# Token choice layer of a four-layer kernel: second weights in four pieces, another place for two stores and for the split of x

## The chip, the cores and the metric

The program runs on 1 core of one Trainium2 chip. The metric is the device time of one execution in microseconds (us).

## The reference, cut to what matters

Four layers work on x of shape (8, 1024, 256), float32: windowed attention, a token choice layer with 64 small experts, linear attention, and attention with nested widths; each is followed by a residual sum and a layer norm. The change touches the second one only:

```python
grouped = x.reshape(x.shape[:-2] + (-1, 16, d))          # groups of 16 tokens
logits = jnp.einsum('...btd,des->...btes', grouped, controller) + tie
perm = (logits == jnp.max(logits, axis=-3, keepdims=True)).astype(x.dtype)
sel = jnp.einsum('...btd,...btes->...besd', grouped, perm)   # 64 experts pick one token each of a group
inner = jax.nn.relu(jnp.einsum('...besd,desf->...besf', sel, f1) + bias)
inter = jnp.einsum('...besf,esfd->...besd', inner, f2)       # f2: 64 experts of 64 x 256
out = jnp.einsum('...besd,...btes->...btd', inter, perm)     # back to the tokens
x = _layernorm(x + out)
```

## The kernel before

The engines are TensorE (PE), VectorE (DVE), ScalarE (ACT) and GpSimd (POOL). SP issues the DMAs of this layer, in its program order; a wait in front of one DMA holds up all behind it. Every engine walks through one list of steps, `steps`, written out by hand. A step is (offset, kind, number); in the turn B of the list it works on the pair of sequences X = B + offset. There are four pairs, X = 0 to 3, and turns for B from -1 to 4; a step whose pair does not exist is left out. What a step does on each engine stands in the functions `piece`. An engine runs its parts in the order of the list, so the list sets the order on all five.

A pair has 2048 tokens in 128 groups. The 64 experts are worked through in two halves of 32. For one half:

- `pT` (L1252) transposes the one-hot choice; ACT copies it to `chosen` (L1123).
- `sel` (L1261) multiplies x by the choice. x is split into two parts, `hi` and `lo`, both in the buffer `hl`: ACT writes hi = x rounded (L1131), then lo = x - hi (`low`, L927) follows, on POOL for pairs 1 to 3. For pair 0 DVE makes the first half of lo and POOL the second, at the end of the layer ahead.
- `h` (L1267) applies the first weights f1, ACT (L1159) and DVE (L1192) add the bias and clip into `hidden`; two `h` steps a half.
- `inter` (L1274), eight steps a half, applies f2 to four experts each. ACT (L1163) and DVE (L1197) evacuate half each into `wide`, and SP stores each of these outputs, 0.5 MB, to DRAM (L1062).
- `gather` (L1075) reads the half's eight outputs back in another layout, in four pieces of 1 MB, once all eight stores have landed.
- `out` (L1281), four steps a half, brings them back to the tokens; DVE adds them to x (L1207) and for half 1 takes the statistics (L176).

PE's results go to four PSUM slots in rotation; a slot is reused when its readers are done.

After half 1 of a pair, `aggregate` (DVE L182, then POOL L187 and L189, the reciprocal root) and `rescale` normalise x: DVE scales the second eight tiles in four steps, POOL the first eight in one (L932). POOL makes the copies of step (0, "spread", 1) (L1103) before it. `store` (L1079) writes a half of x to the next layer, 1 MB each: store 1 needs DVE's tiles, store 0 POOL's.

The next pair is prepared beside half 1 of the present one: `load` of x in two halves (L1056), `xT` (PE L957, copies L975), `logits` (PE L969), then on DVE the tie (L949), the maximum (L938) and the comparison with it (L940), for half 0 at once and for half 1 in step `second`. `spread` 0 (ACT L1143) lays the choice out for `pT`.

The tile names of the profile are those of a buffer's first name: `l0f_f` in the layer is f2 (in DRAM `in_dram`), `l0f_hl` is hi and lo, `x` in DRAM is the layer's input or output.

f2 has one buffer of 2 MB for 32 experts, `f2`. Half 0 of a pair needs the first 32 experts, half 1 the others, so it is loaded twice a pair, each time in one DMA (L1069), when the eighth `inter` of the half before has been filled. `inter` 0 and `inter` 8 wait for it.

Of the kernel before, what the change touches and what calls it, by code (L numbers as in the profile page):

```python
# [49 lines left out]


def tokens(dram, b):

    return dram[bass.ds(b, 1), :, :].rearrange("o (t p) d -> p (o t) d", p=P)


def alone(eng):


    eng.nop(nofuse=True)  # L60


def wait_alone(eng, sem, value):
    eng.wait_ge(sem, value)
    alone(eng)
# [754 lines left out]
def token_choice_layer(nc, block, semaphores, kept, x_in, y_out, controller, f1_in, f2_in, f1_bias, tie_in, ident_in, scratch):  # L820
# [13 lines left out]
    PAIRS = EH // 2  # L834
    HB = 8
    IN = PAIRS // 2
    NC = TT // 4
    NB = NSEQ // 2
    def selection(half):
        out = [(0, "pT", half * TP)]  # L840
        for tp in range(TP):
            if tp + 1 < TP:
                out.append((0, "pT", half * TP + tp + 1))
            out.append((0, "sel", half * TP + tp))
        return out

    def experts(half):
        h, o = [(0, "h", 2 * half + n) for n in range(2)], [(0, "inter", IN * half + n) for n in range(IN)]
        return [h[0], o[0], o[1], h[1]] + o[2:]

    def combination(offset, half):
        return [(offset, "out", NC * half + n) for n in range(NC)]

    s, e, late = selection(0), experts(0), combination(-1, 1)
    turned = selection(1)[:2]
    steps = [(-1, "gather", 1), (0, "f2", 0)] + s[2:] + e[:1] + late + [(-1, "aggregate", 0), (0, "spread", 1)]
    steps += e[1:4] + [(-1, "rescale", 0), e[4], (-1, "rescale", 1), e[5], (-1, "rescale", 2), e[6], (-1, "rescale", 3), e[7], turned[0],
                       e[8], turned[1], e[9]]
    steps += [(-1, "store", 1), (-1, "store", 0), (0, "gather", 0), (1, "load", 0), (1, "load", 1), (0, "f2", 1)]
    s, e, early = selection(1), experts(1), combination(0, 0)  # L860
    steps += s[2:] + e[:1] + early + [(1, "xT", n) for n in range(4)] + [(1, "logits", 0), (1, "spread", 0)]
    steps += e[1:4] + [(1, "second", 0)] + e[4:6] + [(1, "hi", 0), (1, "lo", 0)] + e[6:8]
    steps += [(1, "hi", 1), (1, "lo", 1), (1, "pT", 0), e[8], (1, "pT", 1), e[9]]
    slotted = ("xT", "logits", "pT", "sel", "h", "inter", "out")

    sb, _, sem = allocators(nc, kept, semaphores, "l0f", "right")
    consts = sem("consts"); setup = sem("setup")
    ln = LayerNorm(sb, sem, "ln", setup, 1, TT)
    spread = sb("spread", [P, 2, NQ, J, G])
    x = sb("x", [P, 2, TT, D])  # L870
    wide = sb("wide", [P, 2 * TT, D])
    xT = wide[:, 0:TT, :].rearrange("p t d -> p (t d)").rearrange("p (c t) -> p c t", c=CH)
# [8 lines left out]
    hi, lo = (hl[:, part, :, :].bitcast(f32r) for part in range(2))  # L881
    hidden = sb("hidden", [P, 8, NG])
    f2 = sb("f2", [P, PAIRS, D])
    f1 = sb("f1", [P, CH, E, F])
    schedule = Schedule(steps, slotted, None, NB)
    arrived = schedule.arrived

    def signal(name, per, step=1):
        return Signal(sem(name), per, step)

    f1_loaded = sem("f1_loaded"); f2_loaded = signal("f2_loaded", 2, 16)
    x_loaded = [signal(f"x_loaded{n}", 1, 16) for n in range(2)]; stored = [signal(f"stored{n}", 1, 16) for n in range(2)]
    filled = {o: signal(f"filled{o - schedule.offsets[0]}", sum(s[0] == o for s in schedule.plan))
              for o in schedule.offsets}
# [8 lines left out]
    left = [signal(f"left{half}", IN, 16) for half in range(2)]  # L903
    normed = [signal(f"normed{n}", NT) for n in range(2)]
    back = [signal(f"back{i}", 2, 16) for i in range(NC)]
# [13 lines left out]
    f2_rows = f2_in.rearrange("(p e) f d -> (e f) p d", e=2)  # L919
# [57 lines left out]
    class First:  # L977
# [10 lines left out]
            return buffer[(slice(None),) * (len(names.split()) + 1)].rearrange(f"p {names} -> p ({names})")  # L988

        def start_sp(self, sp):  # L990
            for s in (f2_loaded, *x_loaded, *stored, *left, *back):
                s.start(sp)

        def start_pool(self, pool):
# [47 lines left out]
    def programs(tail, sb, ps):  # L1042
# [3 lines left out]
        @block.sync  # L1046
        def _(sp):
            def piece(step, X, seq, n, B):
                _, kind, i = step
                part = slice(NT * i, NT * i + NT)  # L1050
                if kind == "load" and X:
                    if X == 1:
                        tail.wait_stored(sp)
                    stored[i].wait(sp, X - 2)
                    alone(sp)
                    x_loaded[i].by(sp.dma_start(x[:, X % 2, part, :], tokens(x_in, 2 * X + i)))  # L1056
                if kind == "inter":
                    half, n = divmod(i, IN)
                    inter_even.wait(sp, X, i + 1)
                    alone(sp)  # L1060
                    inter_odd.wait(sp, X, i + 1)
                    left[half].by(sp.dma_start(scratch[half, :, 4 * n:4 * n + 4, :], wide[:, 4 * n:4 * n + 4, :]))  # L1062
                if kind == "f2":
                    schedule.wait_filled(sp, X if i else X - 1, ("inter", IN - 1 if i else 2 * IN - 1))
                    alone(sp)
                    if X == 0 and i == 0:
                        for sem, count in tail.read:
                            wait_alone(sp, sem, count)
                    f2_loaded.by(sp.dma_start(f2[:, :, :], f2_rows[:, PAIRS * i:PAIRS * i + PAIRS, :]))  # L1069
                if kind == "gather":  # L1070
                    wait_alone(sp, left[i].sem, (X + 3) * IN * 16)
                    rows = scratch[i, :, :, :].rearrange("(q j) e d -> (j e) q d", j=J)
                    for n in range(NC):
                        q = slice(NQ // NC * n, NQ // NC * (n + 1))
                        back[n].by(sp.dma_start(wide[:, q, :], rows[:, q, :]))  # L1075
                if kind == "store":
                    normed[i].wait(sp, X)
                    alone(sp)
                    stored[i].by(sp.dma_start(tokens(y_out, 2 * X + i), x[:, X % 2, part, :]))  # L1079

            schedule.loop(sp, piece)

        @block.gpsimd
# [131 lines left out]
        def _(pe):  # L1215
# [6 lines left out]
            def piece(step, X, seq, n, B):  # L1222
                _, kind, i = step
# [12 lines left out]
                if kind == "inter":  # L1236
                    hidden_even.wait(pe, X, 2 * i + 2)
                    hidden_odd.wait(pe, X, 2 * i + 2)
                    if i % IN == 0:
                        f2_loaded.wait(pe, X, i // IN + 1)  # L1240
                if kind == "out":
                    back[i % NC].wait(pe, X, i // NC + 1)
                s = schedule.use(pe, X, step, B)
# [4 lines left out]
                if kind == "pT":  # L1248
                    half, tp = divmod(i, TP)
# [26 lines left out]
                if kind == "out":  # L1276
                    half, n = divmod(i, NC)
# [923 lines left out]
```

How the kernel before makes its waits and increments, by code:

```python
def wait_alone(eng, sem, value):  # L63
    eng.wait_ge(sem, value)
    alone(eng)
# [37 lines left out]
    def wait(self, eng, block, n=None):  # L103
        eng.wait_ge(self.sem, self.count(block, n))
# [27 lines left out]
    def wait_free(self, pe, b, key):  # L133
        old = self.before(key)
        if old is not None:
            for sem, per_sequence, position in self.emptied(old):
                pe.wait_ge(sem, b * per_sequence + position)
# [44 lines left out]
    def reciprocal_root(self, pool, b, use):  # L184
        pool.wait_ge(self.aggregated, self.count(b, use) * self.tiles)
        pool.tensor_scalar(self.mv[:, :, 1], self.mv[:, :, 1], LN_EPS, None, ALU.add).then_inc(self.var_ready, 1)
        pool.wait_ge(self.var_ready, self.count(b, use))
        pool.tensor_tensor(self.rstd[:, :], self.mv[:, :, 1], self.half[:, :], ALU.pow).then_inc(self.rstd_ready, 1)
# [45 lines left out]
    def wait_memsets(self, eng):  # L235
        eng.wait_ge(self.setup, 3)
# [15 lines left out]
def negative_mean(pool, ln, to, sems, X):  # L252
    pool.wait_ge(ln.rstd_ready, X + 1)
    pool.tensor_tensor(to[:, :], ln.mv[:, :, 0], ln.rstd[:, :], ALU.mult).then_inc(sems[0], 1)
    pool.wait_ge(sems[0], X + 1)
    pool.tensor_scalar(to[:, :], to[:, :], -1.0, None, ALU.mult).then_inc(sems[1], 1)
# [43 lines left out]
    def use(self, pe, X, step, B):  # L301
# [5 lines left out]
        if i > -4 * size:  # L307
            for sem, count in self.until(B + i // size, self.plan[i % size]):
                pe.wait_ge(sem, count)
        return self.slot_in(B, step)
# [649 lines left out]
    def logits(pe, X, s):  # L960
        if X == 0:
            pe.wait_ge(consts, 16 * NCONST)
        xT_even.wait(pe, X)
```

## Time and profile before

| what | value |
|---|---|
| median of 3 runs | 2532.25 us (2531.35 to 2538.84) |
| the profiled execution: its time | 2531.27 us |
| the profiled execution: span of the core | 2529.4 us |
| token choice layer within the span | about 1030 to 1450 us |
| PE busy over the span | 2190.4 us, 87% |
| DVE, ACT, POOL busy | 1419.5, 994.7, 899.1 us |

The span runs from the first to the last instruction; the execution's own time has 1.9 us more around it. An engine counts as busy while it computes; its waits and the issuing of DMAs do not count.

### The profile page before, as it was taken

How to read it: one execution, taken by the hardware profiler on the slowest of the kernel's cores; microseconds unless marked ns; L12 is line 12 of the kernel's file. 1: busy time of each engine (PE TensorE's matmuls, PEld its weight loads, DVE VectorE, ACT ScalarE, POOL GpSimd, SP SyncE). 2: the span in 40 equal slices, each digit the busy share in tenths (PEclk: the TensorE clock that was granted, in tenths of full speed). 3: DMA queues.
4: the chain of work that ended last, by engine and by line, in shares of the span. 5: the costliest groups of instructions: out<-in, count | busy, mean ns of one | idle time of the engine just before them, and what ended most of it. 6: DMA issues, size and time to landing. Idle time of an engine off the chain costs nothing.

```text
span 2529.4 us, 42561 instructions
## 1 busy us (share of the span) xinstructions
PE 2190.4 (87%) x17140; PEld 1376.5 (54%) x17140; DVE 1419.5 (56%) x2526; ACT 994.7 (39%) x1450; POOL 899.1 (36%) x573
## 2 busy tenths in 40 slices
PE   4899999999999999788878599999588888888885
PEld 2445555555555555566667456776355555555553
DVE  3545555555555555556466444554466777676772
ACT  1233333333333333545435144333144554554443
POOL 4222222222222220103123022201457877787784
PEclk7899999999999999999999899999799999999997
DMA  6555555555555554367877722201663455445411
GB/s 150 117 118 110 109 110 110 109 115 110 113 110 116 110 107 89 125 212 261 280 248 266 263 92 67 67 26 33 190 161 99 114 145 145 132 113 146 128 35 50
DMA packets 227971, 328.81 MB, mean 130 GB/s; under 512 B 14544, under 2 KB 167104, under 8 KB 227520
## 3 DMA queue, kind: packets, MB, share of 16 engines
q1 hardware_dynamic: 220784, 321.49, 48.4%
q10 hardware_dynamic: 6992, 4.60, 0.6%
q8 instruction: 137, 2.24, 0.4%
q14 instruction: 58, 0.48, 0.1%
HBM read 197.46 MB, written 127.93 MB: 129 GB/s over the span
## 4 chain that ended last, share of the span: by engine, by line
PE 57%; DVE 16%; POOL 7%; DMA 7%; ACT 5%; issue 4%; SPq 3%; ACTq 1%; POOLq 0%; DVEq 0%
PE l0a_slot L775 8%; PE l0a_slot L785 7%; PE l0a_O L710 5%; DVE l1f_rowmax L1972 4%; PE l1a_slot L1568 4%; PE l0a_slot L752 4%; POOL l1f_added L1849 4%; ACT l0f_f L590 2%; PE l0a_slot L757 2%; PE l1a_slot L1559 2%; PE l0a_slot L803 2%; POOL l1f_added L1851 2%; DVE l0f_hidden L655 2%; DMA l0f_f<-in_dram 2%; PE l1f_slot L2103 2%
## 5 line engine op out<-in xcount | busy, mean ns | idle before, releaser
L590 ACT ACTIVATE l0f_f<-l0a_slot 128x1024 f32<-128x1024 f32 (+1 forms) x256 | 248.3, 971 | 337.8 <-PE l0a_slot L775 189.0
L655 DVE TENSOR_REDUCE l0f_hidden<-l0a_slot 128x4 f32<-128x1024 f32 (+1 forms) x256 | 293.4, 1156 | 115.5 <-PE l0a_slot L785 112.5
L1921 ACT ACTIVATE l1f_probs<-l1f_slot 128x1024 f32<-128x1024 f32 x240 | 243.8, 1022 | 271.9 <-PE l1f_slot L2103 265.2
L1849 POOL TENSOR_TENSOR l1f_added<-l1f_probs 128x1024 f32<-128x1024 f32 x117 | 277.3, 2370 | 152.4 <-ACT l1f_probs L1921 152.4
L1972 DVE TENSOR_REDUCE l1f_rowmax<-l1f_slot 128x1 f32<-128x1024 f32 x240 | 287.2, 1216 | 65.6 <-PE l1f_slot L2094 64.9
L775 PE MATMUL l0a_slot<-l0f_hidden 128*128 128x512 bf16 (+1 forms) x1024 | 296.0, 374 | 13.3 <-DMA l0f_hl<-qk_rows 9.0
L549 POOL TENSOR_TENSOR l0f_x<-l0f_x 128x512 f32<-128x512 f32 x32 | 40.7, 1272 | 540.3 <-DVE l0f_x L639 540.3
L2103 PE MATMUL l1f_slot<-l1f_Qs,l1f_Ks 128*128 128x256 f32 x960 | 173.9, 306 | 39.0 <-DVE l1f_lo L1962 14.8
L2103 PEld LDWEIGHTS l1f_slot<-l1f_Qs,l1f_Ks 128*128 128x128 f32 x960 | 146.3, 198 | 96.9 <-DVE l1f_rowmax L1972 33.9
L2094 PE MATMUL l1f_slot<-l1f_Ks,l1f_Qs 96*128 96x512 f32 x480 | 175.9, 451 | 25.7 <-DVE l1f_rowmax L1972 18.4
L710 PE MATMUL l0a_O<-l0f_f,l0f_wide 128*32 128x128 f32 x3840 | 156.4, 279 | 10.5 <-issue 10.5
L1851 POOL TENSOR_TENSOR l1f_added<-l1f_added 128x512 f32<-128x512 f32 x117 | 149.6, 1279 | 9.2
L2027 PE MATMUL l1f_os<-l1f_probs,l1f_V 128*32 128x256 f32 x1920 | 145.4, 396 | 0.1
L785 PE MATMUL l0a_slot<-l0a_Qs,l0f_hl 49*128 49x256 f32 (+1 forms) x1024 | 127.1, 327 | 18.3 <-ACT l0f_f L590 17.1
L785 PEld LDWEIGHTS l0a_slot<-l0f_hl,l0a_Qs 48*128 48x128 f32 x1024 | 77.7, 188 | 103.8 <-issue 103.8
L785 PEld LDWEIGHTS l0a_slot<-l0a_Qs,l0f_hl 49*128 49x128 f32 x1024 | 76.8, 186 | 103.3 <-issue 68.3
L752 PE MATMUL l0a_slot<-l0f_x,l0f_spread 128*128 128x512 f32 x256 | 123.5, 629 | 6.6 <-DVE l0f_spread L623 5.1
L785 PE MATMUL l0a_slot<-l0f_hl,l0a_Qs 48*128 48x256 f32 (+1 forms) x1024 | 128.7, 330 | 0.0
L710 PEld LDWEIGHTS l0a_O<-l0f_f,l0f_wide 128*32 128x32 f32 x3840 | 90.3, 109 | 64.6 <-issue 37.4
L775 PEld LDWEIGHTS l0a_slot<-l0f_hidden 128*128 128x128 bf16 x1024 | 63.8, 98 | 96.5 <-issue 61.7
L2094 PEld LDWEIGHTS l1f_slot<-l1f_Ks,l1f_Qs 96*128 96x128 f32 x480 | 78.3, 199 | 68.8 <-issue 30.0
L601 ACT COPY l0f_f<-l0a_O 128x512 f32<-128x512 f32 x64 | 37.4, 585 | 196.1 <-PE l0a_O L710 196.0
(194 smaller groups left out, 3770.2 us busy)
## 6 DMA issues: line engine op xcount, KB each, us to landing
expert_outputs<-l0f_wide SPq DMA_DIRECT2D x64, 512.0 KB, 3.3
l0f_wide<-expert_outputs SPq DMA_DIRECT2D x32, 1024.0 KB, 10.9
l1f_Ks<-kq_rows SPq DMA_DIRECT2D x48, 512.0 KB, 8.2
l0a_Qs<-qk_rows SPq DMA_DIRECT2D x90, 256.0 KB, 7.8
l0f_hl<-qk_rows SPq DMA_DIRECT2D x90, 256.0 KB, 14.5
l0f_f<-in_dram SPq DMA_DIRECT2D x10, 2048.0 KB, 14.7
qk_rows<-l0f_wide SPq DMA_DIRECT2D x32, 512.0 KB, 2.8
qk_rows<-l0f_x SPq DMA_DIRECT2D x32, 512.0 KB, 4.2
```

The source lines that it names most:

```text
L590: exp_ready.by(act.activation(probs[:, t % 2, HG * g:HG * g + HG, 0:reach, :], s[:, :, 0:reach, :], ACT.Exp, scale=SCALE))
L655: max_ready.by(dve.reduce_max(rowmax[:, t, :, 2 * g:2 * g + 2], s[:, :, :, first:2 * P], AX))
L710: last = mm(O[t % 2][32 * j:32 * j + 32, g, :], V[:, tile - a, HG * g + j, :], probs[:, (t - a) % 2, HG * g + 2 * (j % 2) + j // 2, a, :], ...
L752: last = mm(s[:, BW * r:BW * r + BW], w[:, c, P * r:P * r + P], xT[:, n, c, :], start=c == 0, stop=c == CH - 1)
L775: at_end = mm(o[:, half, :, reach, :], ident16[:, :], table[:, reach, :].unsqueeze(1).broadcast_to([P, 2, wide, P]), start=not mask_ends, ...
L785: last = mm(o[:, half, j, reach, :].rearrange("p a q -> p (a q)"), left[r, 2 * g + j, here], right[r, 2 * g + j, moving], start=mask_ends ...
L1849: halved.by(pool.tensor_tensor(added[:, u, :], probs[:, 0, u, :], probs[:, 1, u, :], ALU.add))
L1851: add_done.by(pool.tensor_tensor(added[:, u, 0:SKT * QW], added[:, u, 0:SKT * QW], added[:, u, SKT * QW:HKT * QW], ALU.add))
L1921: exp_done.by(act.activation(probs[:, half, u - FIRST[b], :], s[:, :], ACT.Exp, scale=SCALE))
L1972: max_done.by(dve.reduce_max(rowmax[:, i:i + 1], s[:, :], AX))
L2094: last = mm(s[:, 512 * half:512 * half + 512], Qs[0:96, parity, u, P * t:P * t + P], Ks[0:96, parity, UNITS[u][0], 512 * half:512 * half + ...
L2103: last = mm(s[:, QW * j:QW * j + QW], Ks[:, parity, UNITS[u][0], P * kt:P * kt + P], Qs[:, parity, u, :], start=True, stop=True)
```

## The change

f2 is loaded in four pieces of 0.5 MB a half, step numbers 0 to 3 for half 0 and 4 to 7 for half 1, each with a semaphore of its own (`f2_loaded[part]`). A piece may be loaded when the second `inter` step that reads its predecessor in the buffer has been filled, and every second `inter` step waits for its piece. Two pieces of each half go out among the `inter` steps of the half before, the other two behind the gather (and behind the loads of x). The stores of the old pair move: store 1 from behind `inter` 7 to before `inter` 6 (`e[8]`), store 0 to before `inter` 7 (`e[9]`). The steps `hi` and `lo` of the next pair move from between the `inter` steps of half 1 to directly behind `logits`, before `spread` 0.

```diff
--- before.py
+++ after.py
@@ -853,14 +853,14 @@
 
     s, e, late = selection(0), experts(0), combination(-1, 1)
     turned = selection(1)[:2]
-    steps = [(-1, "gather", 1), (0, "f2", 0)] + s[2:] + e[:1] + late + [(-1, "aggregate", 0), (0, "spread", 1)]
-    steps += e[1:4] + [(-1, "rescale", 0), e[4], (-1, "rescale", 1), e[5], (-1, "rescale", 2), e[6], (-1, "rescale", 3), e[7], turned[0],
-                       e[8], turned[1], e[9]]
-    steps += [(-1, "store", 1), (-1, "store", 0), (0, "gather", 0), (1, "load", 0), (1, "load", 1), (0, "f2", 1)]
+    steps = [(-1, "gather", 1), (0, "f2", 2), (0, "f2", 3)] + s[2:] + e[:1] + late + [(-1, "aggregate", 0), (0, "spread", 1)]
+    steps += e[1:4] + [(0, "f2", 4), (-1, "rescale", 0), e[4], (-1, "rescale", 1), e[5], (0, "f2", 5), (-1, "rescale", 2), e[6],
+                       (-1, "rescale", 3), e[7], turned[0], (-1, "store", 1), e[8], turned[1], (-1, "store", 0), e[9]]
+    steps += [(0, "gather", 0), (1, "load", 0), (1, "load", 1), (0, "f2", 6), (0, "f2", 7)]
     s, e, early = selection(1), experts(1), combination(0, 0)
-    steps += s[2:] + e[:1] + early + [(1, "xT", n) for n in range(4)] + [(1, "logits", 0), (1, "spread", 0)]
-    steps += e[1:4] + [(1, "second", 0)] + e[4:6] + [(1, "hi", 0), (1, "lo", 0)] + e[6:8]
-    steps += [(1, "hi", 1), (1, "lo", 1), (1, "pT", 0), e[8], (1, "pT", 1), e[9]]
+    steps += s[2:] + e[:1] + early + [(1, "xT", n) for n in range(4)] + [(1, "logits", 0)]
+    steps += [(1, "hi", 0), (1, "lo", 0), (1, "hi", 1), (1, "lo", 1), (1, "spread", 0)]
+    steps += e[1:4] + [(1, "f2", 0), (1, "second", 0)] + e[4:6] + [(1, "f2", 1)] + e[6:8] + [(1, "pT", 0), e[8], (1, "pT", 1), e[9]]
     slotted = ("xT", "logits", "pT", "sel", "h", "inter", "out")
 
     sb, _, sem = allocators(nc, kept, semaphores, "l0f", "right")
@@ -888,7 +888,7 @@
     def signal(name, per, step=1):
         return Signal(sem(name), per, step)
 
-    f1_loaded = sem("f1_loaded"); f2_loaded = signal("f2_loaded", 2, 16)
+    f1_loaded = sem("f1_loaded"); f2_loaded = [signal(f"f2_loaded{n}", 2, 16) for n in range(4)]
     x_loaded = [signal(f"x_loaded{n}", 1, 16) for n in range(2)]; stored = [signal(f"stored{n}", 1, 16) for n in range(2)]
     filled = {o: signal(f"filled{o - schedule.offsets[0]}", sum(s[0] == o for s in schedule.plan))
               for o in schedule.offsets}
@@ -988,7 +988,7 @@
             return buffer[(slice(None),) * (len(names.split()) + 1)].rearrange(f"p {names} -> p ({names})")
 
         def start_sp(self, sp):
-            for s in (f2_loaded, *x_loaded, *stored, *left, *back):
+            for s in (*f2_loaded, *x_loaded, *stored, *left, *back):
                 s.start(sp)
 
         def start_pool(self, pool):
@@ -1061,12 +1061,13 @@
                     inter_odd.wait(sp, X, i + 1)
                     left[half].by(sp.dma_start(scratch[half, :, 4 * n:4 * n + 4, :], wide[:, 4 * n:4 * n + 4, :]))
                 if kind == "f2":
-                    schedule.wait_filled(sp, X if i else X - 1, ("inter", IN - 1 if i else 2 * IN - 1))
+                    half, part = divmod(i, 4)
+                    schedule.wait_filled(sp, X if half else X - 1, ("inter", 2 * part + 1 if half else IN + 2 * part + 1))
                     alone(sp)
                     if X == 0 and i == 0:
                         for sem, count in tail.read:
                             wait_alone(sp, sem, count)
-                    f2_loaded.by(sp.dma_start(f2[:, :, :], f2_rows[:, PAIRS * i:PAIRS * i + PAIRS, :]))
+                    f2_loaded[part].by(sp.dma_start(f2[:, 4 * part:4 * part + 4, :], f2_rows[:, 4 * i:4 * i + 4, :]))
                 if kind == "gather":
                     wait_alone(sp, left[i].sem, (X + 3) * IN * 16)
                     rows = scratch[i, :, :, :].rearrange("(q j) e d -> (j e) q d", j=J)
@@ -1236,8 +1237,8 @@
                 if kind == "inter":
                     hidden_even.wait(pe, X, 2 * i + 2)
                     hidden_odd.wait(pe, X, 2 * i + 2)
-                    if i % IN == 0:
-                        f2_loaded.wait(pe, X, i // IN + 1)
+                    if i % 2 == 0:
+                        f2_loaded[i % IN // 2].wait(pe, X, i // IN + 1)
                 if kind == "out":
                     back[i % NC].wait(pe, X, i // NC + 1)
                 s = schedule.use(pe, X, step, B)
```

## Rows read from the trace of the kernel before

**Rows 1.** The page, busy time of the engines over the whole span.

```profile
PE 2190.4 (87%) x17140; PEld 1376.5 (54%) x17140; DVE 1419.5 (56%) x2526; ACT 994.7 (39%) x1450; POOL 899.1 (36%) x573
```

**Rows 2.** Busy times in one stretch; the last number is GB/s of the DMA queues.

```profile
1102.50:1122.00 19.50, 15.26 (x151) 11.11 (x150) 8.44 (x15) 3.92 (x11) 0.00 (x0) 0.91 1.07 348
```

**Rows 3.** Waits of PE from 1030 to 1440 us: total us, times, longest.

```profile
PE l0f_slot L1274 <- DMA l0f_f<-in_dram: 10.8, 3, 4.1
...
PE l0f_slot L1261 <- ACT l0f_chosen L1123: 7.7, 4, 2.4
```

**Rows 4.** Timeline of PE: start us, us; in brackets the idle time before.

```profile
1122.67 1.94 PE L957 MATMUL l0f_slot<-l0f_ident,l0f_x 128*128 128x128 f32 x16 [1.07 <-DMA l0f_x<-x]
...
1220.87 1.94 PE L957 MATMUL l0f_slot<-l0f_ident,l0f_x 128*128 128x128 f32 x16 [1.07 <-DMA l0f_x<-x]
...
1243.96 1.75 PE L1261 MATMUL l0f_slot<-l0f_chosen,l0f_hl 128*128 128x256 f32 x8 [2.36 <-ACT l0f_chosen L1123]
...
1269.59 2.00 PE L1274 MATMUL l0f_slot<-l0f_f,l0f_hidden 64*128 64x256 f32 x16 [2.56 <-DMA l0f_f<-in_dram]
...
1316.11 1.94 PE L957 MATMUL l0f_slot<-l0f_ident,l0f_x 128*128 128x128 f32 x16 [1.08 <-DMA l0f_x<-x]
...
1411.19 3.47 PE L1274 MATMUL l0f_slot<-l0f_f,l0f_hidden 64*128 64x256 f32 x16 [4.12 <-DMA l0f_f<-in_dram]
```

**Rows 5.** Timeline of the queue SP, the issues of the gathers.

```profile
1100.68 5.65 SPq L1075 DMA_DIRECT2D l0f_wide<-expert_outputs  x4
...
1195.63 9.77 SPq L1075 DMA_DIRECT2D l0f_wide<-expert_outputs  x4
...
1247.59 5.44 SPq L1075 DMA_DIRECT2D l0f_wide<-expert_outputs  x4
...
1291.04 9.76 SPq L1075 DMA_DIRECT2D l0f_wide<-expert_outputs  x4
```

**Rows 6.** Timeline of POOL.

```profile
1056.61 4.84 POOL L927 TENSOR_TENSOR l0f_hl<-l0f_x,l0f_hl 128x2048 fp32r<-128x2048 f32 x1 [12.98 <-ACT l0f_hl L1131]
...
1062.72 2.81 POOL L1103 COPY l0f_spread<-l0f_choice 32x512 f32<-32x512 f32 x4
...
1182.09 10.02 POOL L932 TENSOR_SCALAR l0f_x<-l0f_x,l0f_ln_mv,l0f_ln_rstd 128x256 f32<-128x256 f32 x8 [0.24 <-POOL l0f_spread L1103]
...
1239.33 9.06 POOL L927 TENSOR_TENSOR l0f_hl<-l0f_x,l0f_hl 128x2048 fp32r<-128x2048 f32 x2 [47.22 <-ACT l0f_hl L1131]
...
1280.55 9.95 POOL L932 TENSOR_SCALAR l0f_x<-l0f_x,l0f_ln_mv,l0f_ln_rstd 128x256 f32<-128x256 f32 x8 [0.24 <-POOL l0f_spread L1103]
```

**Rows 7.** Timeline of DVE.

```profile
1043.73 1.38 DVE L195 TENSOR_SCALAR l0f_x<-l0f_x,l0a_ln_mv,l0a_ln_rstd 128x256 f32<-128x256 f32 x4 [1.55 <-POOL l0a_ln_rstd L189]
...
1054.76 2.29 DVE L927 TENSOR_TENSOR l0f_hl<-l0f_x,l0f_hl 128x2048 fp32r<-128x2048 f32 x1 [3.31 <-ACT l0f_hl L1131]
...
1062.87 2.81 DVE L195 TENSOR_SCALAR l0f_x<-l0f_x,l0a_ln_mv,l0a_ln_rstd 128x256 f32<-128x256 f32 x4 [2.76 <-POOL l0a_ln_rstd L189]
...
1229.93 0.69 DVE L940 TENSOR_TENSOR l0f_choice<-l0f_choice,l0f_best 128x512 f32<-128x512 f32 x1
...
1272.92 1.17 DVE L182 BATCH_NORM_AGGREGATE l0f_ln_mv<-l0f_ln_stats 128x2 f32<-128x6 f32 x16
...
1285.85 0.69 DVE L1197 COPY l0f_wide<-l0f_slot 128x512 f32<-128x512 f32 x1 [1.25 <-PE l0f_slot L1274]
```

**Rows 8.** Timeline of ACT.

```profile
1050.27 2.54 ACT L1143 COPY l0f_spread<-l0f_choice 32x512 f32<-32x512 f32 x4 [1.70 <-DVE l0f_choice L940]
...
1230.71 2.53 ACT L1143 COPY l0f_spread<-l0f_choice 32x512 f32<-32x512 f32 x4 [7.73 <-DVE l0f_choice L940]
...
1237.32 1.93 ACT L1131 CAST l0f_hl<-l0f_x 128x2048 fp32r<-128x2048 f32 x1
```

**Rows 9.** DMA issues from 1030 to 1440 us: count, size, us to landing.

```profile
expert_outputs<-l0f_wide SPq DMA_DIRECT2D x64, 512.0 KB, 3.3
...
x<-l0f_x SPq DMA_DIRECT2D x6, 1024.0 KB, 6.5
```
## The prediction

> **What bounds the kernel now.** I read the page first: TensorE (PE) is busy for 87% of the whole span [rows 1], so a gain must come from stretches where PE stands still. The change touches the token choice layer alone, about 1030 to 1450 us. The table of waits for this layer comes next [rows 3]: PE waits 10.8 us for the second weights (f2) and 7.7 us in front of the selection matmuls, besides its waits for gathered outputs and for x. These are the waits that the change aims at; which of them carry time is read from the timelines [rows 4 to 8].
>
> I cut the layer at the moments at which the second half of x lands and PE turns it: 1122.67, 1220.87 and 1316.11 [rows 4]. One full turn, 1220.87 to 1316.11, is 95.2 us and has four links. (a) 53.2 us until VectorE (DVE) has aggregated the statistics of the old pair, 1272.92+1.17 = 1274.1 [rows 7]. (b) 16.4 us until GpSimd (POOL) ends its root, its copies and eight rescaled tiles, 1280.55+9.95 = 1290.5 [rows 6]. (c) 0.5 us until the queue issues gather 0 at 1291.04 [rows 5]. (d) 25.1 us until x has landed behind it [rows 4]. The turn before it took 98.2 us, since gather 0 left 3.5 us after POOL's end (1192.1 to 1195.63) and x 25.2 us later [rows 4 to 6]. The last turn runs from 1316.11 to 1411.19, where the first output matmul of half 1 waits 4.12 us for f2 [rows 4].
>
> On an idle queue gather 0 is quicker: issued at 1100.68, with x there at 1122.67, it is 22.0 us for 6 MB [rows 4, 5]. At the 348 GB/s that the queue then moves [rows 2], 1 MB takes 3.0 us; so the fourth piece of a gather lands 22.0-6.0 = 16.0 us after the issue, and the backlog of the two y stores is worth 25.1-22.0 = 3.1 us.
>
> **The change, part by part.**
>
> **f2 in pieces, half 0.** PE no longer waits for f2 before expert output 0 (2.56 us at 1269.59, 10.8 us in three waits [rows 3, 4]). I cost this gain at nothing by itself: the outputs' evacuations stand behind the aggregate in DVE's order, and the aggregate runs until 1274.1, after f2 is there [rows 7]. It needs the gathered outputs, not f2. If DVE were free it would be worth up to 2.6 us a turn. The 4.12 us before 1411.19 are on the path and counted below. With them goes the half-speed stretch behind that wait: sixteen matmuls took 3.47 us there, against 2.00 us after the shorter wait at 1269.59 [rows 4]; -1.6 us with what follows it.
>
> **f2 in pieces, the load added elsewhere.** Two pieces of 0.5 MB now go out between the eight output stores of each half, 1.5 us each. The first falls into the gap left by the h step and costs nothing; the second falls among stores back to back and makes the gather 1.5 us later. For pair 0, half 0 that is +1.5 us on x (0 to +3). For the other halves it is in the numbers below.
>
> **x split behind the logits, pair 0.** ScalarE (ACT) is idle 1.70 us before its spread, which starts at 1050.27, and makes hi only after its 2.54 us [rows 8]. Now hi comes first, from 1048.6, so done at 1050.4 and 1052.3. DVE makes lo 0 (2.29 us) from 1051.5 to 1053.8; POOL's lo 1 follows, and its end moves from 1061.45 to 1058.4 if POOL must let DVE finish, or to 1057.3 if not [rows 6, 7]. POOL's root, the last normalisation of the layer ahead and the selection's evacuations follow that end: -3.0 us (-4.1 without a conflict; 0 if another chain takes over).
>
> **x split behind the logits, pairs 1 to 3.** ACT stands idle 7.73 us before its spread at 1230.71 [rows 8]; hi 0 and hi 1 (1.93 us each) fit there, from 1223.0 to 1226.8. So 3.9 us leave the loaded part of ACT's order, and selection no longer waits for lo 0, which POOL now ends at 1239.33+4.53 = 1243.9, just where PE resumes at 1243.96 [rows 4, 6]. That wait of 2.36 us is gone, and it is the gain one would expect.
>
> But POOL's two lo's now run from 1225.0 to 1229.5 and from there to 1234.1. DVE's comparison (L940: two operands, both in SBUF) wants to start at 1229.93 [rows 7], 0.4 us into the second. The trace has no such comparison under a lo. Nearest is the normalisation L195: four tiles take 1.38 us with POOL idle, and 2.81 us while POOL makes four copies, which take 2.81 us too [rows 6, 7]. The two engines took turns, one whole instruction each. The other overlap is lo 1 of pair 0, started 0.44 us before DVE's lo 0 ended: 4.84 us instead of 4.53 [rows 6, 7]. Bounds for L940: no delay, or the rest of lo 1, 4.2 us. I take 4.2 us, by L195. The Trainium skill (SBUF — State Buffer, Who interferes with whom) says the same of just this pair of instructions: a DVE instruction with two SBUF inputs and a GpSimd instruction that reads SBUF exclude each other for a whole instruction, and the later one waits. By it, too, the delay is 4.2 us; were it wrong here, the sum would be that of rival 1.
>
> With 4.2 us the first stores of half 1 are 4.2 us later. The f2 piece adds 1.5 us; gather 1 goes out near 1253.4 instead of 1247.59 [rows 5]. Its fourth piece lands 16.0 us later, at 1269.4; PE's last combination ends near 1271.3, and DVE's add (1.2), statistics (1.4) and aggregate (1.2) at 1275.1. Link (a) is then +1.0 us in each of three turns. Without the delay, ACT's shorter order brings the last store forward and gather 1 goes out near 1249.3: fourth piece 1265.3, aggregate end 1271.0, so -3.1 us a turn.
>
> **y stores ahead of the last outputs.** Store 1 needs DVE's tiles only and moves forward freely. Store 0 needs POOL's eight tiles, which end at 1290.5 [rows 6], while DVE has evacuated output 7 at 1285.85+0.69 = 1286.5 [rows 7], as POOL's end hangs on the aggregate alone. The queue works in order: behind store 0 stand now the store of output 7, gather 0, both loads of x and the last f2 pieces, and PE waits for them. Before, output 7 had landed when POOL finished. Now 1 MB and 0.5 MB go out at POOL's end, and gather 0 must wait until the latter has landed. A 1 MB y store lands after 6.5 us, an output store after 3.3 us [rows 9]; with 1.5 us of data for output 7 the pair takes between 6 and 9 us. I take 7.5. After POOL's end x then needs 7.5+22.0 = 29.5 us, against 28.8 before in the first turn (+0.7) and 25.6 in the second (+3.9). In the third, half 1 starts when the fourth combination (1.95 us) is through: 7.5+16.0+1.95 = 25.4 against some 25.5 (-0.1; this contains the 4.12 us wait for f2). Together +4.5 us; each us on the 7.5 counts three times. The Trainium skill (DMA: Bandwidth & Descriptors, Queues, rings and completion order) adds that a DMA's semaphore increment lands only after all earlier writes of that engine; by it the store of output 7 can't be seen before store 0 has been written, which keeps the lower end near 6.
>
> **Sum:** -3.0 (pair 0) +1.5 (first gather) +3x1.0 +4.5 -1.6 = +4.4 us. The profiled execution took 2531.27 us (span 2529.4 and 1.9 around it), 1.0 below the median of 2532.25. So 2535.7 for that execution, and 2536.6 as a median.
>
> **The rivals.**
> 1. *No delay of L940* (it is served beside lo 1, or comes 0.4 us before it). Then -4.1+1.5-3x3.1+4.5-1.6 = -9.0: 2523.2 us, faster. For it: no row shows this pair of instructions, and the margin is small. Against it: the L195 and lo 1 rows.
> 2. *The store of output 7 lands later*: queued behind f2 piece 5, store 1, output 6 and store 0, it needs 10 us after POOL's end instead of 7.5. Price 3x2.5: 2544.1 us, slower. It decides from about 8.6 us on, since +4.4+3x1.1 is 7.6 us. For it: outputs 2 to 6, the f2 piece and store 1 are 4 MB, 12 us of data asked for in the 11 us before POOL's end. Against it: a median landing of 6.5 us that already has backlog in it [rows 9].
> 3. *The change does what it says*: every f2 wait and selection wait is gain, 10.8+7.7 us: 2513.8 us. Against it: both end behind work of DVE and POOL. It has no chance of its own beyond 0.03.
>
> **How the numbers follow.** 0.3% of the time, 7.6 us, is about what a measurement tells from no change. Forecast 0.50 (its own range 2530 to 2543), rival 1 0.27, rival 2 0.20, rival 3 0.03. Of the forecast 0.42 stays within the bound and 0.06 lies above it; rival 1 gives 0.17 faster and 0.10 within; rival 2 0.18 slower; the rest is split. Faster 0.21, same 0.54, slower 0.25. The range reaches to both rivals: 2520 to 2545.
>
> **What would show it.** Right: L940 ends near the end of POOL's second lo in pairs 1 to 3, and ACT's spread follows; no f2 wait on PE; on the queue a gap before output 7's store until POOL's last tile, and gather 0 some 7 us after POOL's end; selection of pair 0 about 3 us earlier. Wrong: L940 at its old distance from the logits; aggregates 3 us earlier; gather 0 within 5 us of POOL's end; or DVE's normalisation ahead of pair 0 not moved.

## The result, and the profile after

| | median | runs | ratio to before, 95% interval |
|---|---|---|---|
| before | 2535.01 us | 8 (2530.90 to 2538.84) | |
| after | 2543.94 us | 8 (2539.32 to 2544.74) | 1.0035 [1.0024, 1.0045] |

The change makes the kernel 8.9 us slower, 6 to 11 us by the interval. The profiled execution after has a span of 2541.5 us. The numbers of the lines below 859 are one higher in the kernel after (L1274 is L1275, L1281 is L1282, L1131 is L1132).

The page of the kernel after, the engines' busy time, answers to [rows 1]:

```profile
PE 2196.1 (86%) x17140; PEld 1373.5 (54%) x17140; DVE 1432.1 (56%) x2526; ACT 994.7 (39%) x1450; POOL 900.2 (35%) x573
```

PE runs the same 17140 matmuls and is busy 5.7 us longer with them; the other 6.4 of the 12.1 us more of span are waits. DVE is busy 12.6 us longer, and that is not work either: 11.6 us of it are three rows of one instruction, shown below. PE's waits from 1030 to 1440 us answer to [rows 3]:

```profile
PE l0f_slot L1282 <- DMA l0f_wide<-expert_outputs: 31.9, 23, 2.7
PE l0f_slot L1275 <- ACT l0f_wide L1164: 10.4, 3, 3.5
```

The wait for f2 has gone, and so has the one in front of the selection, as the change promises. In their place stand a wait for ACT's evacuations, 3.5 us in each of three turns, and more waiting for the gathered outputs: before it was 24.0 us, but 11.6 of them in one wait at 1436.47, whose counterpart of 12.2 us ends at 1445.55 in the kernel after, outside this window, so 12.4 us have become 31.9. The timelines of one turn show where each comes from. First DVE, with the pair's first maximum, the comparison and the aggregate ([rows 7] before):

```profile
1229.36 0.68 DVE L938 TENSOR_REDUCE l0f_best<-l0f_choice 128x32 f32<-128x512 f32 x1
1230.07 4.54 DVE L940 TENSOR_TENSOR l0f_choice<-l0f_choice,l0f_best 128x512 f32<-128x512 f32 x1
...
1275.54 1.17 DVE L182 BATCH_NORM_AGGREGATE l0f_ln_mv<-l0f_ln_stats 128x2 f32<-128x6 f32 x16
```

The comparison L940 took 0.69 us before and takes 4.54 us now. I read this as waiting inside the row and not as slower computing; e1 and e9 below test it. POOL in the same stretch ([rows 6] before), from pair 0's lo on:

```profile
1050.22 5.80 POOL L927 TENSOR_TENSOR l0f_hl<-l0f_x,l0f_hl 128x2048 fp32r<-128x2048 f32 x1 [8.62 <-ACT l0f_hl L1132]
...
1225.01 9.05 POOL L927 TENSOR_TENSOR l0f_hl<-l0f_x,l0f_hl 128x2048 fp32r<-128x2048 f32 x2 [34.05 <-ACT l0f_hl L1132]
...
1283.09 10.04 POOL L932 TENSOR_SCALAR l0f_x<-l0f_x,l0f_ln_mv,l0f_ln_rstd 128x256 f32<-128x256 f32 x8 [0.24 <-POOL l0f_spread L1104]
```

The two lo's run from 1225.01 to 1234.06. The comparison begins at 1230.07, some 0.5 us after the start of the second lo, and its row ends at 1234.61, 0.55 us after the end of that lo. Behind it ACT's spread and evacuations ([rows 8] before):

```profile
1223.02 3.70 ACT L1132 CAST l0f_hl<-l0f_x 128x2048 fp32r<-128x2048 f32 x2
1234.70 2.53 ACT L1144 COPY l0f_spread<-l0f_choice 32x512 f32<-32x512 f32 x4 [7.97 <-PE l0f_slot L1275]
1237.26 1.07 ACT L1164 COPY l0f_wide<-l0f_slot 128x512 f32<-128x512 f32 x2
```

hi now takes its 3.70 us in ACT's idle time, but the spread starts at 1234.70, 3.9 us later after x than before (1230.71). PE, turn by turn ([rows 4] before):

```profile
1221.01 1.94 PE L957 MATMUL l0f_slot<-l0f_ident,l0f_x 128*128 128x128 f32 x16 [1.08 <-DMA l0f_x<-x]
...
1238.09 4.64 PE L1275 MATMUL l0f_slot<-l0f_f,l0f_hidden 64*128 64x256 f32 x24 [3.45 <-ACT l0f_wide L1164]
...
1323.19 1.94 PE L957 MATMUL l0f_slot<-l0f_ident,l0f_x 128*128 128x128 f32 x16 [1.07 <-DMA l0f_x<-x]
```

The bracket at 1238.09 is the wait that has come: PE stands 3.45 us for an evacuation behind the spread. The queue ([rows 5] before):

```profile
1254.79 5.42 SPq L1076 DMA_DIRECT2D l0f_wide<-expert_outputs  x4
...
1287.62 0.58 SPq L1080 DMA_DIRECT2D x<-l0f_x  x1
...
1293.19 0.37 SPq L1080 DMA_DIRECT2D x<-l0f_x  x1
1293.66 0.87 SPq L1062 DMA_DIRECT2D expert_outputs<-l0f_wide  x1
1301.00 5.35 SPq L1076 DMA_DIRECT2D l0f_wide<-expert_outputs  x4
```

Gather 1 goes out at 1254.79, 33.8 us after x has landed at 1221.01 (26.7 before). Store 0 goes out when POOL has finished its eighth tile at 1293.13, the store of output 7 at 1293.66 behind it, and gather 0 only at 1301.00, 7.9 us after POOL's end (0.5 before). The chain of waits links these up:

```profile
1245.64 0.70 DVE l0f_wide L1198
1246.35 1.16 SPq L1062
...
1247.60 7.12 DMA expert_outputs<-l0f_wide
...
1257.44 13.29 DMA l0f_wide<-expert_outputs
...
1270.78 1.97 PE l0f_slot L1282 x16
1272.77 1.23 DVE l0f_x L1208
...
1283.09 10.05 POOL l0f_x L932 x8
...
1293.66 7.28 DMA expert_outputs<-l0f_wide
...
1311.33 11.72 DMA l0f_x<-x
```

The last output of half 1 takes 7.12 us to land, the last output of half 0 7.28 us; POOL's tiles stand between the aggregate and the queue. The start of the last half, without the f2 wait that stood before it:

```profile
1421.29 2.00 PE L1275 MATMUL l0f_slot<-l0f_f,l0f_hidden 64*128 64x256 f32 x16
1423.22 3.71 PE L1268 MATMUL l0f_slot<-l0f_sel,l0f_f 128*64 128x128 f32 x64
```

### The profile page after: what moved, and what is told of

Same layout as the page of the kernel before. It is cut to its first block, busy times and chain, and to the rows that moved or that the text cites. A ratio compares the mean times of both kernels' runs of the same rounds, so it can differ in the third digit from the quotient of the medians.

```text
span 2541.5 us, 42619 instructions
## 1 busy us (share of the span) xinstructions
PE 2196.1 (86%) x17140; PEld 1373.5 (54%) x17140; DVE 1432.1 (56%) x2526; ACT 994.7 (39%) x1450; POOL 900.2 (35%) x573
## 4 chain that ended last, share of the span: by engine, by line
PE 56%; DVE 15%; POOL 9%; DMA 7%; ACT 5%; issue 4%; SPq 3%; ACTq 1%; POOLq 0%; DVEq 0%
PE l0a_slot L775 8%; PE l0a_slot L785 7%; PE l0a_O L710 5%; DVE l1f_rowmax L1973 4%; PE l1a_slot L1569 4%; PE l0a_slot L752 4%; POOL l1f_added L1850 4%; DMA l0f_wide<-expert_outputs 3%; ACT l0f_f L590 2%; PE l0a_slot L757 2%; DMA expert_outputs<-l0f_wide 2%; PE l1a_slot L1560 2%; PE l0a_slot L803 2%; POOL l1f_added L1852 2%; DVE l0f_hidden L655 2%
## 5 line engine op out<-in xcount | busy, mean ns | idle before, releaser
L2104 PEld LDWEIGHTS l1f_slot<-l1f_Qs,l1f_Ks 128*128 128x128 f32 x960 | 145.3, 196 | 95.4 <-DVE l1f_rowmax L1973 32.5
```

The source lines that it names most:

```text
L2104: last = mm(s[:, QW * j:QW * j + QW], Ks[:, parity, UNITS[u][0], P * kt:P * kt + P], Qs[:, parity, u, :], start=True, stop=True)
```

## The experiments

All turns were cut as in the prediction. (a) is x landed to aggregate end, (c) POOL's end to gather 0, (d) gather 0 to the next x; (b), aggregate to POOL's end, is 16.2 to 16.5 us in every kernel. "Pair 0" is from the start of the last projection of the layer ahead (L803) to x of pair 1, "g1" from x landed to the issue of gather 1. The turn shown is the second, in us; each number is a difference of two starts or ends in the one profiled execution of that kernel, which can lie some us beside the median (e2: 2540.5 against 2534.9, e7: 2523.3 against 2527.1). The medians are of 4 to 12 runs; each ratio is to runs of the kernel before that were taken beside that kernel, with medians of 2533.0 to 2535.0 us.

| kernel | pair 0 | g1 | (a) | (c) | (d) | median | ratio to before |
|---|---|---|---|---|---|---|---|
| before | 73.95 | 26.7 | 53.2 | 0.5 | 25.1 | 2535.0 | 1 |
| after | 71.96 | 33.8 | 55.7 | 7.9 | 22.2 | 2543.9 | 1.0035 |
| e5 split alone | 70.72 | 31.8 | 53.4 | 7.7 | 24.7 | 2545.8 | 1.0045 [1.0032, 1.0058] |
| e6 stores alone | 73.25 | 26.6 | 51.8 | 8.7 | 21.1 | 2541.2 | 1.0027 [1.0016, 1.0038] |
| e7 f2 alone | 75.46 | 29.5 | 51.8 | 2.8 | 24.3 | 2527.1 | 0.9974 [0.9963, 0.9984] |
| e4 split in old place | 75.56 | 30.2 | 53.2 | 7.6 | 22.3 | 2538.5 | 1.0010 [0.9999, 1.0022] |
| e1 lo 1 waits | 72.20 | 30.4 | 52.2 | 7.8 | 21.9 | 2531.8 | 0.9984 [0.9973, 0.9994] |
| e2 store 0 back | 72.00 | 34.7 | 57.1 | 4.8 | 23.3 | 2534.9 | 0.9997 [0.9985, 1.0009] |
| e3 both | 72.49 | 30.1 | 51.9 | 5.3 | 22.1 | 2523.4 | 0.9947 [0.9930, 0.9964] |
| e9 lo 1 after first comparison | 72.32 | 30.2 | 51.8 | 5.4 | 21.8 | 2522.0 | 0.9952 [0.9935, 0.9969] |
| e8 both stores behind | 72.64 | 29.7 | 51.8 | 3.3 | 23.6 | 2521.8 | 0.9954 [0.9941, 0.9967] |
| e10 one f2 piece early | 70.80 | 28.3 | 50.2 | 3.3 | 22.5 | 2510.0 | 0.9906 [0.9891, 0.9921] |
| e11 same, both stores behind | 70.77 | 27.9 | 49.8 | 1.2 | 24.7 | 2513.4 | 0.9922 [0.9907, 0.9937] |
| e12 e10 with old split | 72.47 | 28.3 | 53.1 | 3.8 | 22.2 | 2524.3 | 0.9962 [0.9948, 0.9976] |

My theory after the result: two costs, the comparison standing outside POOL's second lo, in link (a), and the queue standing in front of output 7's store, in link (c). The rivals: each long row or wait costs nothing, since something else sets the turn.

**e1: the second lo waits for both comparisons.** An edit on the kernel after, in POOL's piece:

```diff
                 if kind == "lo" and X:
+                    if i:
+                        choice_ready.wait(pool, X)
                     low(pool, X, i)
```

> The kernel after, with one wait more: GpSimd starts the second half of lo only when VectorE has made both comparisons of the pair (the first half of lo starts as early as in the kernel after). Theory (the comparison of 4.54 us is VectorE standing outside GpSimd's second lo, and it delays everything of half 1 behind it): the first comparison is back at 0.69 us, gather 1 goes out 4 to 6 us earlier after x, and each of three turns is 3 to 5 us shorter, so 2543.9 - 12 = about 2532 us, ratio to the kernel before 0.996 to 1.001. Rival A (a long row that costs nothing, since the stores of output 7 behind store 0 set the turn): unchanged, ratio 1.003 to 1.004. Rival B (the moved wait only shifts the collision to the second comparison or delays the selection): comparison rows of over 1 us appear elsewhere, ratio above 1.002.

All comparisons take 0.69 us again. Gather 1 goes out 3.4 us earlier in the turn shown (4.5 and 3.9 in the others), link (a) is 3.5 us shorter (55.7 to 52.2), and the time falls to 2531.8 us, 12 us below the kernel after. The collision cost that much; rivals A and B fall.

**e2: store 0 behind inter 7 again.** On the kernel after:

```diff
-    ... e[8], turned[1], (-1, "store", 0), e[9]]
-    steps += [(0, "gather", 0), ...
+    ... e[8], turned[1], e[9]]
+    steps += [(-1, "store", 0), (0, "gather", 0), ...
```

> The kernel after, with store 0 behind inter 7 again, directly ahead of gather 0; store 1 stays ahead of inter 6. Theory (the queue stands 5 us before the store of output 7 until GpSimd's last tile, then waits for its landing behind 1 MB): gather 0 goes out under 2 us after GpSimd's end instead of 7.8 to 8.2; x lands some 23 to 25 us after that end instead of 30.1, so three turns are each 4 to 6 us shorter: about 2529 us, ratio 0.996 to 1.000. Rival A (the data queue is full anyway, so store 0 costs its 3 us behind the gather what it costs ahead of it): at most 2 us a turn, ratio 1.001 to 1.003.

A gain of 9 us over the kernel after, a part of it from (c): 4.8 us instead of 7.9. That is not the "under 2 us" of the theory. The second turn's (c) and (d) together are 28.0 us against 30.1, the 2 us a turn that rival A allowed at most, though its ratio (1.001 or more) was too high: the gather does not go out when POOL is through, but when output 7 has landed, 8.06 us after its store at 1291.05. The whole 9 us can't be followed in the profile, since the profiled execution was the slowest of the twelve.

**e3: both edits.**

> Both edits on the kernel after: the second half of lo waits for both comparisons, and store 0 stands behind inter 7. Theory: the two costs lie in different links of the turn (x to the aggregate, and GpSimd's end to x) and add up, so 2543.9 - 12 - 15 = about 2517 us, ratio 0.991 to 0.996. Rival (they lie in series on one resource, the DMA queue, and removing one exposes the other's cost elsewhere): no better than the better of the two alone, ratio 0.997 or more.

2523.4 us, a ratio of 0.9947, within the expected band, though 6 us above the expected 2517, which had counted 15 us for the stores where e2 gives 9; (a) shows the one gain and (c) the other. They add up (12.1 and 9.0 us alone, 20.5 us together) and the rival falls. The chain of waits of this kernel, at output 7, shows what is left in (c):

```profile
1278.45 8.31 DMA expert_outputs<-l0f_wide
...
1286.83 0.37 SPq L1076
```

Output 7 takes 8.31 us to land. Ahead of it on the queue are an f2 piece and store 1, behind it store 0.

**e4: the split back in its old place,** all else as after. The edit puts `(1, "hi", 0), (1, "lo", 0)` behind e[4:6] and the other two behind e[6:8] again.

> The kernel after, with the steps hi and lo back between the inter steps of half 1. Theory: the comparisons take 0.69 us again, but ScalarE's 3.9 us of hi and the wait of the selection for lo are back too, and so is the later start of pair 0 (3.4 us). Each of three turns 1 to 3 us shorter than in the kernel after, minus 3.4 us at pair 0: 2537 to 2543 us, ratio 1.001 to 1.003. Rival (the early split gained nothing at all, its cost was pure): ratio 0.998 or below.

2538.5 us, as expected: comparisons of 0.69 us, but pair 0 is 3.6 us later (75.56 against 71.96).

**e5: the early split alone,** on the kernel before.

> The kernel before with one part of the change alone: hi and lo of the next pair directly behind logits. Theory: the first comparison takes 4.5 us in pairs 1 to 3, gather 1 goes out 4 us later after x and f2 lands behind it; pair 0 starts 3.4 us earlier. 2535 to 2541 us, ratio 1.000 to 1.002. Rival (the early split is a gain in itself and only the mixture with f2 and the stores hurts): ratio 0.998 or below.

The largest miss: 2545.8 us, no faster than the whole change (the intervals, 1.0032 to 1.0058 and 1.0024 to 1.0045, overlap). The theory priced it too low, and the rival had the wrong sign. PE's timeline of this kernel, the fourth combination of the half is the first row:

```profile
1268.34 1.95 PE L1281 MATMUL l0f_slot<-l0f_wide,l0f_spread 128*64 128x256 f32 x16 [1.07 <-DMA l0f_wide<-expert_outputs]
1274.38 3.79 PE L1274 MATMUL l0f_slot<-l0f_f,l0f_hidden 64*128 64x256 f32 x16 [4.09 <-DMA l0f_f<-in_dram]
```

The gather is 5.1 us later after x than before, and f2, still in one DMA behind it, lands 4 us after PE has finished the combinations. The matmuls behind that wait are slow too: sixteen in 3.79 us against 2.00 us, with a granted clock of 0.66 from 1274.4 to 1282.6, so a part of it at the lower level of 1.2 GHz. Output 7 is evacuated at 1292.9, after POOL's end at 1290.5, and (c) is 7.7 us although no store stands in its way. In the kernel before, PE resumed at 1269.59 behind its f2 wait of 2.56 us, output 7 was evacuated at 1286.5 and (c) was 0.5 us. I read it so that POOL's tiles hid the lateness there and no longer hide it here; no run separates the late gather from the late f2.

**e6: the two stores alone,** on the kernel before.

> The kernel before with one part alone: store 1 ahead of inter 6, store 0 ahead of inter 7. Theory: the queue stands in front of the store of output 7 until GpSimd's last tile and the gather goes out 7 us after it; x lands 29 to 30 us after GpSimd's end (28.8 and 25.6 before). Together +6 to +10 us: 2541 to 2545 us, ratio 1.002 to 1.004. Rival (the y stores' 3.1 us of backlog saved behind the gather pay for it, as the run with store 0 moved back suggests with 2 us a turn): ratio 0.999 to 1.0015.

2541.2 us, as the theory has it: (c) is 8.7 us, and (d) is 4.0 us shorter without the backlog. In the first turn (c) is 9.7 us. One thing was not in the theory: (a) is 51.8 us in the turn shown and 53.2 in the other two, with the split in its old place in all three. PE waits about 2.36 us in front of the selection in each; behind that wait eight matmuls took 1.19 us in the turn shown:

```profile
1248.14 1.19 PE L1261 MATMUL l0f_slot<-l0f_chosen,l0f_hl 128*128 128x256 f32 x8 [2.36 <-ACT l0f_chosen L1123]
```

In the kernel before they took 1.75 us at 1243.96 [rows 4] and the next eight 2.06 us, with a granted clock of 0.57 from 1243.9 to 1247.9 against 1.00 in e6 from 1248.1 to 1252.1. The two levels of 1.2 and 2.4 GHz thus make (a) 53.0 to 53.2 or 51.8 to 51.9 us where the selection decides; no run tells why the clock fell in some turns and not in others.

**e7: f2 in pieces alone,** on the kernel before.

> The kernel before with one part alone: f2 in four pieces a half. Theory: no wait for f2, the last turn some 4 us and the stretch behind it 1.6 us shorter; against that 1.4 us on the first gather and about 1 us a turn for the piece among the stores. 2528 to 2534 us, ratio 0.9975 to 1.000. Rival (every wait for f2 of the kernel before is gain, 12.6 us with the two that end with it): ratio 0.9955 or below.

2527.1 us, a gain of 0.26%, just below the 2528 to 2534 expected. The rival, that each wait for f2 is gain, would have given 0.9955 or below and falls. In this execution the clock held behind all three waits for the selection (eight matmuls in 1.19 us), and (a) is 0.8 to 1.4 us shorter than before; that part need not be f2's doing. The three parts alone are +0.45, +0.27 and -0.26%, together +0.46% against the measured +0.35%: nearly additive.

**e8: lo 1 waits, both y stores behind inter 7.**

> The kernel after with the second lo waiting for both comparisons and both y stores behind inter 7, as in the kernel before. In the run with store 0 alone put back the gather still went out 5.3 us after GpSimd's end, as the store of output 7 took 8.3 us to land with 1 MB of store 1 and an f2 piece ahead of it. Theory (that backlog is store 1's, and it costs the same 3 us ahead of the gather as behind it): the gather goes out 1 to 3 us after GpSimd's end, x lands 24 to 25 us behind it, and the time is that of the run with both fixes, 2521 to 2526 us, ratio 0.9945 to 0.9965. Rival (store 1 ahead is a gain of its own): ratio above 0.9965.

2521.8 us, the same as e3. Behind output 7's store, store 1 takes 2.0 us off (c) (5.3 to 3.3) and adds 1.5 us to (d) (22.1 to 23.6); its place does not measurably matter so long as POOL is not in front of the queue.

**e9: as e3, but the second lo waits for the first comparison alone** (`choice_ready.wait(pool, X, 1)`).

> The kernel with both fixes, but the second lo waits for the first comparison alone, so it starts just when that comparison ends and is over before the second one wants to start (GpSimd's lo takes 4.5 us, the comparisons lie 6.9 us apart). Theory (only the overlap of a comparison with a running lo costs): all comparisons 0.69 us, the time that of the run with both fixes, 2519 to 2527 us, ratio 0.993 to 0.997. Rival (any lo on GpSimd in this stretch slows VectorE, which also adds, evacuates and clips there): rows of VectorE under the second lo longer than before, ratio above 0.998.

POOL and DVE of this kernel:

```profile
1218.43 4.55 POOL L927 TENSOR_TENSOR l0f_hl<-l0f_x,l0f_hl 128x2048 fp32r<-128x2048 f32 x1 [31.14 <-ACT l0f_hl L1134]
1224.26 4.55 POOL L927 TENSOR_TENSOR l0f_hl<-l0f_x,l0f_hl 128x2048 fp32r<-128x2048 f32 x1 [1.28 <-DVE l0f_choice L940]
```

```profile
1223.49 0.69 DVE L940 TENSOR_TENSOR l0f_choice<-l0f_choice,l0f_best 128x512 f32<-128x512 f32 x1
...
1230.35 0.69 DVE L940 TENSOR_TENSOR l0f_choice<-l0f_choice,l0f_best 128x512 f32<-128x512 f32 x1
```

The second lo starts 0.08 us after the first comparison ends. It overlaps two of DVE's copies (1.28 us) and six of its clips (1.71 us), which read PSUM and take just as long as in e3; it is over at 1228.81, before DVE's second maximum and comparison. 2522.0 us, the time of e3: the overlap with the comparison costs, the overlap with the copies and clips does not.

**e10: as e3, with one f2 piece early instead of two.** Pieces 1 and 5 go behind the gather (and the loads of x) with the other two:

```diff
-    steps = [(-1, "gather", 1), (0, "f2", 2), (0, "f2", 3)] + ...
+    steps = [(-1, "gather", 1), (0, "f2", 1), (0, "f2", 2), (0, "f2", 3)] + ...
-    ... e[5], (0, "f2", 5), (-1, "rescale", 2) ...
+    ... e[5], (-1, "rescale", 2) ...
-    ... (1, "load", 1), (0, "f2", 6), (0, "f2", 7)]
+    ... (1, "load", 1), (0, "f2", 5), (0, "f2", 6), (0, "f2", 7)]
-    ... e[4:6] + [(1, "f2", 1)] + e[6:8] ...
+    ... e[4:6] + e[6:8] ...
```

> The kernel with both fixes, and of the four f2 pieces of a half only the first goes out among the inter steps ahead; the second goes behind the gather with the other two. Theory (a piece among back-to-back stores delays the landing of the last store by its 1.5 us, and nobody needs the second piece before 20 us after the gather's issue): gather 1 goes out 1 to 1.5 us earlier after x, gather 0 as much earlier after GpSimd's end, six to seven such places: 2514 to 2520 us, ratio 0.992 to 0.995. Rival (the queue has slack there, the landing of the last store is set by its evacuation): unchanged, 2523 us, ratio 0.9945 to 0.996.

2510.0 us, 13 us below e3 and better than expected. Pair 0, g1 and (c) are 1.7, 1.8 and 2.0 us shorter (1.4 and 2.2, 1.4 and 1.7 in the other turns), 12 us in seven places: there a piece of 0.5 MB among back-to-back stores cost 1.4 to 2.2 us, about its 1.5 us of transfer or somewhat more. At output 7 the chain of waits has 6.33 us instead of 8.31:

```profile
1184.58 6.33 DMA expert_outputs<-l0f_wide
...
1190.97 0.37 SPq L1076
```

**e11: the same with both y stores behind inter 7.**

> The same single early piece, with both y stores behind inter 7. Theory: output 7's store has neither store 1 nor a piece ahead of it and lands by GpSimd's end, so the gather goes out 1 to 2 us after it; the y stores' 2 MB then delay x by 3 us. 2514 to 2520 us, no measurable difference from the run with store 1 ahead. Rival (the y stores ahead are worth their 1 MB): 3 us or more slower than that run.

(c) falls to 1.2 us and (d) rises by 2.2. 2513.4 us is 3.4 us above e10, but the intervals overlap, so whether store 1 ahead is worth anything stays open.

**e12: e10 with the split in its old place.**

> The fastest kernel so far (one f2 piece early, store 0 behind inter 7, the second lo waiting) with hi and lo back between the inter steps of half 1. It tells what the early split is worth once its collision is out of the way. Theory (it saves the selection's wait for lo, ScalarE's 3.7 us among the evacuations, and 3.4 us at pair 0): pair 0 starts 3.4 us later and x to the aggregate is 1 to 2 us longer in three turns: 6 to 9 us slower than that kernel, 2516 to 2519 us, ratio 0.993 to 0.9945. Rival (the early split is worth only its 3.4 us at pair 0): ratio 0.9915 to 0.9925.

This kernel leaves the added wait of the second lo out, and needs none: lo starts at 1233.92, after both comparisons (the second ends at 1232.06). Both prices were too low: 14 us slower than e10 (10.2 us by the spans of the two profiles). Pair 0 is 1.7 us later, not 3.4. (a) is 1.7, 3.0 and 3.6 us longer in the three turns, 53.1 us instead of 50.2 in the one shown, since the selection waits for lo again while gather 1 would be ready, and behind that wait PE starts at its lower clock in two of the three turns:

```profile
1238.54 1.33 PE L1263 MATMUL l0f_slot<-l0f_chosen,l0f_hl 128*128 128x256 f32 x8 [2.36 <-ACT l0f_chosen L1125]
...
1239.95 2.06 PE L1263 MATMUL l0f_slot<-l0f_chosen,l0f_hl 128*128 128x256 f32 x8
```

## Why the prediction was right, and where its sizes were off

The measured +8.9 us lies on the side that was forecast (+4.4), just beyond what I had called no change, and is twice the forecast. That the time, 2543.9 us, lies inside the range of 2520 to 2545 is partly luck: it is above the forecast's own 2530 to 2543 and equals the figure of rival 2 (2544.1), whose mechanism did not come true; and 2.8 us of the distance to the forecast 2536.6 are that the kernel before has a median of 2535.0 over 8 runs and had 2532.25 over 3. The mechanisms of the forecast were right, and one term of its sum, link (a), was too small by 5 us. The steps, in the order of the sum; the two profiles are aligned at the start of L803 (1048.72 before, 1046.69 after).

- **f2, half 0: nothing.** Right. The waits for f2 are gone and the aggregate ends no earlier. e7 gives f2 alone 7 us; in its profile the last turn is 3.9 us and the stretch behind it 1.6 us shorter, as the prediction had it.
- **f2 pieces among the stores: +1.5 at the first gather.** Right at pair 0: the step to x of pair 1 moved by -2.0 us in the whole change against -1.5 forecast, and by +1.5 with the pieces alone (e7). For gather 1 it was too little: with the pieces alone it goes out 2.0, 2.8 and 3.7 us later after x than before.
- **Pair 0: -3.0.** The step with the delay was right: lo 1 of POOL starts at 1050.22, 1.41 us before the end of DVE's lo 0 (1051.63), and its row is 5.80 us, 1.27 more than the 4.53 alone. Selection's third matmul group starts 3.4 us earlier after L803.
- **The comparison: 4.2 us in three turns.** Right in mechanism and nearly in size: 4.54 us for a row of 0.69, thus 3.85 us of delay, ended by POOL's second lo. The Trainium skill (SBUF — State Buffer, Who interferes with whom) is borne out in both orders: POOL stood outside DVE in pair 0, DVE outside POOL in the others. No run takes one operand out of SBUF, so that two SBUF inputs are the condition is the page's word; that DVE's copies and clips from PSUM do not collide with a lo is shown by e9.
- **Link (a): +1.0 a turn.** This is the term that was mis-sized: +2.9, +2.5 and +2.8 us. Gather 1 went out 33.8 us after x, not 32.5; its last store took 7.12 us to land, with 3 MB of outputs and a piece issued within 6 us. The prediction had put the first of the two pieces at nothing and the second at 1.5 us. The pieces alone (e7) move gather 1 by 2.8 us in this turn, 1.3 us more, and that is the 1.3 us between 32.5 and 33.8; one piece less (e10) gives 1.8 us back. Which of the two pieces takes the surplus, no run tells. Where gather 1 decides, (a) is g1 + 21.6 to 21.9 us in the second turn of after, e1, e3, e5, e9, e10 and e11; where gather 1 comes earlier than the selection allows (before, e4, e6, e12), (a) is 53.1 to 53.2, or 51.8 where the clock held (e6).
- **The stores: +4.5, from 7.5 us in (c).** Right: 8.2, 7.9 and 7.8 us were measured, and x 21.9 and 22.2 us behind the gather (22.0 forecast). e6 has the same delay without the f2 pieces. The rule of the Trainium skill (DMA: Bandwidth & Descriptors, Queues, rings and completion order) that a DMA's semaphore increment lands only after every earlier write of that DMA engine does not contradict it, but no run here can tell it from a queue that is merely full: output 7 took 7.28 us behind store 0 and 8.31 us in e3 with store 0 issued after it.
- **The last turn and its tail: -1.6.** Right: 12.0 us from inter 8 to the end of inter 15's matmuls, 13.7 before.

Summed in order of time (start, three turns, tail): -2.0, +4.2, +6.9, +3.0 and -1.6 are +10.5 us in the profiles, against -1.5, +1.7, +4.9, +0.9 and -1.6 forecast. The missing 6.1 us are 5.1 in (a) (8.1 instead of 3.0) and 1.5 in the other links, less 0.5 at the start. Rival 1 had the alternative right in kind: without the collision (e1) the time is 2531.8 us, a little under before, though not the 2523 that I gave it, as its (a) took the same undersized price of the pieces. Rival 2, a later landing of output 7, came true only for 0.4 of its 2.5 us (7.9 measured, 7.5 forecast, 10 its own). Rival 3's time, 2513.8 us, is about what e10 reaches, but by other edits.

The span of the kernel after is 12.1 us longer, although its layer ahead was 2.0 us shorter. The layer itself makes 10.5 us, and 3.6 us more arise behind it, nearly all in the last layer, which the change does not touch; no run tells why, and the medians (8.9 us) leave no room for it.

## What to carry to other kernels

Before moving work into an engine's idle time, look also at what the others do there that reads SBUF: the new place was free for ACT, but POOL's part of the work, which follows ACT's, met a DVE comparison by 0.5 us. A wait that delays the harmless half of the work turned a loss of 9 us into a time 0.16% below before. In an in-order queue put nothing that waits for a slow engine ahead of something whose landing others need, and don't count a small transfer beside stores at nothing because there is a gap: two pieces of 1.5 us made gather 1 2.0 to 3.7 us later. Price a wait by the link behind it: the f2 wait of 2.56 us went with a (c) of 0.5 us in the kernel before, where POOL was busy longer than the outputs, and the one of 4.09 us with 7.7 us in e5, where it was not.

## What the runs showed of the hardware

- A DVE comparison that meets a running POOL subtraction has a row of 4.53 to 4.54 us in 6 of 6 cases (after, e5) and 4.52 to 4.53 in the 3 of e2: the waiting is inside the row, not in front of it, so the table of waits does not list it.
- An output store of 0.5 MB lands in 2.6 us at best and took 8.31 us in e3 with one 1 MB store ahead and one behind; the store behind was issued 3.2 us later. The longest was 9.13 us, in the first turn of e6, behind both 1 MB stores.
- Behind the same wait of 2.36 us TensorE ran its next matmuls at its full clock in some turns (eight in 1.19 us, granted clock 1.00) and at the lower one in others (up to 2.06 us, 0.57 over 4 us with both levels in it); where the selection decides, a turn is 1.3 us longer by it.
- The kernel of e10, the two fixes and one early piece, runs in 2510.0 us, 0.94% [0.79, 1.09] below the kernel before.
